# Query rotation from an SBUF copy, and the carried attention sums moved behind it, in a transformer layer of eight cores

## What is computed

```
xn = layernorm(x)
Q  = rope(xn @ W_q)            # 16 heads
K  = rope(xn @ W_k)            # 4 heads, each used by 4 query heads
V  = xn @ W_v
attn = softmax(Q K^T / sqrt(128)) V @ W_o
ffn  = (silu(xn @ w_gate * s_gate) * (xn @ w_up * s_up)) @ w_down * s_down   # int8 weights, inner width 8192
out  = x + attn + ffn
```

## Time and profile before

| | us |
|---|---|
| median of the two runs shown | 5281.77 |
| the two runs | 4993.61 and 5569.93 |
| the profiled execution | 4927.06 |
| span of its slowest core (core 7) | 4925.5 |
| spans of its eight cores | 4895.3 to 4925.5 |
| TensorE busy in that span | 4116.9 (84%) |
| VectorE busy | 1008.2 (20%) |
| ScalarE busy | 824.4 (17%) |

### The profile page before, as it was taken

How to read it: one execution, slowest core, us unless ns; L and a number is a source line. 1 busy time by engine, 2 the same in 40 slices (tenths; PEclk the granted TensorE clock), 3 DMA queues, 4 the chain that set the end, 5 groups by cost and what they waited for, 6 DMA issues and landing times.

```text
span 4925.5 us, 43667 instructions; the slowest of 8 cores (4895.3 to 4925.5 us)
## 1 busy us (share of the span) xinstructions
PE 4116.9 (84%) x18032; PEld 1774.3 (36%) x18032; DVE 1008.2 (20%) x1324; ACT 824.4 (17%) x659; POOL 224.7 (5%) x432
## 2 busy tenths in 40 slices
PE   0286666666666766799999999999999999999999
PEld 0032222222222222244444444444444444444444
DVE  2354333343233432111100111100111000111000
ACT  3203333333333333211100011000010000001000
POOL 0000000000000000000000000000000000000000
PEclk9998788887888878899999999999999999999999
DMA  9700000000000000443345633345633355533354
GB/s 144 181 1 12 10 9 11 10 12 11 9 10 11 10 9 5 165 175 152 150 151 180 222 154 154 154 154 185 222 150 150 131 184 192 188 154 154 116 187 149
DMA packets 139171, 545.03 MB, mean 111 GB/s; under 512 B 43824, under 2 KB 68416, under 8 KB 95584
## 3 DMA queue, kind: packets, MB, share of 16 engines
q0 software_dynamic: 60720, 465.67, 27.1%
q1 hardware_dynamic: 78256, 76.56, 6.0%
HBM read 345.06 MB, written 33.55 MB: 77 GB/s over the span
## 4 chain that ended last, share of the span: by engine, by line
PE 76%; ACT 12%; DVE 6%; DMA 3%; issue 2%; DVEq 0%; ACTq 0%; POOL 0%; SPq 0%; POOLq 0%
PE ps_sc L581 18%; PE ps_av L627 18%; PE ps_sc L598 18%; ACT expT L469 11%; PE ps_sc L459 5%; PE ps_sc L406 5%; PE ps_sm L637 4%; PE ps_sm L369 2%; PE ps_av L356 2%; DMA x_t<-x_nat 2%; PE ps_sc L454 2%; DVE rb_sb L380 1%; DMA wv_sb<-wv 1%; ACT sqt L276 1%; PE ps_av L326 1%
## 5 line engine op out<-in xcount | busy, mean ns | idle before, releaser
L581 PE MATMUL ps_sc<-xn_t,wg_sb 128*128 128x512 bf16 x4096 | 927.7, 380 | 25.3 <-DMA xn_t<-xn_scr 25.3
L598 PE MATMUL ps_sc<-xn_t,wu_sb 128*128 128x512 bf16 x4096 | 925.8, 379 | 0.0
L627 PE MATMUL ps_av<-fuse,wd_sb 128*128 128x512 bf16 x4096 | 894.5, 379 | 4.3 <-DVE fuse L607 4.3
L469 ACT ACTIVATE expT<-ps_sc,bias_h,isq_sb 128x2048 bf16<-128x2048 f32 x256 | 526.7, 2057 | 709.4 <-PE ps_sc L454 709.4
L581 PEld LDWEIGHTS ps_sc<-xn_t,wg_sb 128*128 128x128 bf16 x4096 | 401.2, 98 | 510.2 <-issue 28.2
L589 ACT ACTIVATE gate_sb<-ps_sc,sg_sb 128x512 bf16<-128x512 f32 x256 | 175.9, 687 | 2417.2 <-PE ps_sc L581 2417.2
L627 PEld LDWEIGHTS ps_av<-fuse,wd_sb 128*128 128x128 bf16 x4096 | 400.5, 98 | 488.5 <-issue 6.2
L598 PEld LDWEIGHTS ps_sc<-xn_t,wu_sb 128*128 128x128 bf16 x4096 | 400.8, 98 | 483.3
L607 DVE SCALAR_TENSOR_TENSOR fuse<-ps_sc,su_sb,gate_sb 128x512 bf16<-128x512 f32 x256 | 192.2, 751 | 1597.2 <-PE ps_sc L598 1597.2
L459 PE MATMUL ps_sc<-qr,kr 128*128 128x512 bf16 x768 | 269.8, 471 | 192.3 <-ACT expT L469 192.3
L380 DVE RECIPROCAL rb_sb<-ps_sm 128x512 f32<-128x512 f32 x64 | 214.9, 3358 | 877.4 <-PE ps_sm L365 875.8
(11 more groups left out here) (66 smaller groups left out, 1309.7 us busy)
## 6 DMA issues: line engine op xcount, KB each, us to landing
wg_sb<-wg POOLq DMA_DIRECT2D x128, 1024.0 KB, 4.6
wu_sb<-wu POOLq DMA_DIRECT2D x128, 1024.0 KB, 6.6
wd_sb<-wd POOLq DMA_DIRECT2D x64, 2048.0 KB, 7.4
wo_sb<-wo POOLq DMA_DIRECT2D x64, 512.0 KB, 6.7
x_t<-x_nat POOLq DMA_DIRECT2D x16, 1024.0 KB, 11.6
xT_sb<-xT SPq DMA_DIRECT2D x64, 256.0 KB, 6.0
outT<-out_sb SPq DMA_DIRECT2D x64, 256.0 KB, 5.9
wq_sb<-wq POOLq DMA_DIRECT2D x16, 512.0 KB, 5.1
```

What stands on the lines that cost most here:

```text
L469: exp_b[b] = es(lambda s, p=qp, b0=4 * b: s.activation(expT[p][:, b0:b0 + 4, :], ps_sc[:, :, :], AF.Exp, bias=bias_h[:], scale=isq_sb[:]), ...
L581: t_.matmul(PS(b), wg_sb[p][:, d, j:j + 128], xn_t[tp][:, d, :], start=(d == 0), stop=(d == DC - 1)))
L598: t_.matmul(PS(b), wu_sb[p][:, d, j:j + 128], xn_t[tp][:, d, :], start=(d == 0), stop=(d == DC - 1)))
L627: t_.matmul(PS(b), wd_sb[p][:, i, :], fuse[:, i, :], start=(i == 0), stop=(i == IC - 1)))
```

## The change

The query part rotates from a copy in SBUF. After the square, ScalarE copies the projected tile from its PSUM bank into a new bf16 buffer `qps`, and that copy is what frees the bank. VectorE waits for the copy and rotates with a new function `rope_sb`, which does the six operations of `rope` on `qps`. Since its inputs are both in SBUF, the odd half's tables are taken from partitions 64 to 127, so `cos_sb` and `sin_sb` grow to 128 partitions and are loaded twice each. K still uses `rope`.

In the same lines the block that put the carried sums and their epilogue into the query part is gone. `pend` stays set through it, and the score loop, which is not edited, finds it set at q = 0 also.

```diff
-            cos_sb = sba("cos_sb", [64, S], F32)
-            sin_sb = sba("sin_sb", [64, S], F32)
+            cos_sb = sba("cos_sb", [128, S], F32)
+            sin_sb = sba("sin_sb", [128, S], F32)
...
-            dma("y", "cs", lambda y: y.dma_start(cos_sb[:], cosd))
-            dma("y", "cs", lambda y: y.dma_start(sin_sb[:], sind))
+            dma("y", "cs", lambda y: y.dma_start(cos_sb[0:64, :], cosd))
+            dma("y", "cs", lambda y: y.dma_start(cos_sb[64:128, :], cosd))
+            dma("y", "cs", lambda y: y.dma_start(sin_sb[0:64, :], sind))
+            dma("y", "cs", lambda y: y.dma_start(sin_sb[64:128, :], sind))
...
+            qps = sba("qps", [128, 4, 512], BF16)
...
+            def rope_sb(src, dst_e, dst_o, t0):
+                ev(lambda v, p=src, a=t0: v.tensor_mul(
+                    tmp0[:], p[0:64, :], cos_sb[0:64, a:a + TS]))
+                ev(lambda v, p=src, a=t0: v.tensor_mul(
+                    tmp1[:], p[64:128, :], sin_sb[64:128, a:a + TS]))
+                ev(lambda v, d=dst_e: v.tensor_sub(d, tmp0[:], tmp1[:]))
+                ev(lambda v, p=src, a=t0: v.tensor_mul(
+                    tmp0[:], p[0:64, :], sin_sb[0:64, a:a + TS]))
+                ev(lambda v, p=src, a=t0: v.tensor_mul(
+                    tmp1[:], p[64:128, :], cos_sb[64:128, a:a + TS]))
                 return ev(lambda v, d=dst_o: v.tensor_add(d, tmp0[:], tmp1[:]))
...
-                    ew("v", st_, qp)
-                    ew("v", ss, sqd)
-                    qrope[t] = rope(ps_sc[:, t, :],
-                                    qr[0:64, t * TS:t * TS + TS],
-                                    qr[64:128, t * TS:t * TS + TS], t * TS)
-                    psum_free[t] = (sv, qrope[t])
-                    if pend is not None:
-                        emit_avsums_batch(pend, t)
-                        if t == NT - 1:
-                            emit_attn_epilogue(pend, pend_head[0],
-                                               pend_head[1])
-                            pend = None
+                    evv = es(lambda s, tt=t: s.copy(
+                        qps[:, tt, :], ps_sc[:, tt, :]), chain=False)
+                    psum_free[t] = (ss, evv)
+                    ew("v", ss, evv)
+                    qrope[t] = rope_sb(qps[:, t, :],
+                                       qr[0:64, t * TS:t * TS + TS],
+                                       qr[64:128, t * TS:t * TS + TS], t * TS)
```

More of the change, by code:

```diff
@@ L259, in rope @@
                 ev(lambda v, p=psum, a=t0: v.tensor_mul(
-                    tmp0[:], p[0:64, :], cos_sb[:, a:a + TS]))
+                    tmp0[:], p[0:64, :], cos_sb[0:64, a:a + TS]))
                 ev(lambda v, p=psum, a=t0: v.tensor_mul(
-                    tmp1[:], p[64:128, :], sin_sb[:, a:a + TS]))
+                    tmp1[:], p[64:128, :], sin_sb[0:64, a:a + TS]))
                 ev(lambda v, d=dst_e: v.tensor_sub(d, tmp0[:], tmp1[:]))
                 ev(lambda v, p=psum, a=t0: v.tensor_mul(
-                    tmp0[:], p[0:64, :], sin_sb[:, a:a + TS]))
+                    tmp0[:], p[0:64, :], sin_sb[0:64, a:a + TS]))
                 ev(lambda v, p=psum, a=t0: v.tensor_mul(
-                    tmp1[:], p[64:128, :], cos_sb[:, a:a + TS]))
+                    tmp1[:], p[64:128, :], cos_sb[0:64, a:a + TS]))
+                return ev(lambda v, d=dst_o: v.tensor_add(d, tmp0[:], tmp1[:]))
+            def rope_sb(src, dst_e, dst_o, t0):
+                ev(lambda v, p=src, a=t0: v.tensor_mul(
+                    tmp0[:], p[0:64, :], cos_sb[0:64, a:a + TS]))
+                ev(lambda v, p=src, a=t0: v.tensor_mul(
+                    tmp1[:], p[64:128, :], sin_sb[64:128, a:a + TS]))
+                ev(lambda v, d=dst_e: v.tensor_sub(d, tmp0[:], tmp1[:]))
+                ev(lambda v, p=src, a=t0: v.tensor_mul(
+                    tmp0[:], p[0:64, :], sin_sb[0:64, a:a + TS]))
+                ev(lambda v, p=src, a=t0: v.tensor_mul(
+                    tmp1[:], p[64:128, :], cos_sb[64:128, a:a + TS]))
                 return ev(lambda v, d=dst_o: v.tensor_add(d, tmp0[:], tmp1[:]))
```

## The result

The changed kernel's profiled execution took 4815.85 us against 4927.06, 111 us or 2.3% less. The changed kernel's executions lie close together (4815.85 to 4819.06 in the first set). Their ratio to those of the kernel before was 0.9738, with a 95% interval of 0.964 to 0.9836, wide because of one execution of the kernel before at 4993.61. That interval alone does not tell 2% from less. So the kernel is faster by 2.2%.

A forecast was written before the change was run, and what follows sets the result against it. VectorE's rotations were taken to bound the attention loop's query part. Per head -6.66 + 0.6 - 0.3 = -6.36 us, -95.4 over 15 heads; with 3 at the start, 4927 - 92 = 4835 us, range 4785 to 4935.

The forecast's parts named there:

- the copy and the rotation from it: In the query part: ScalarE's 64 copies hide in its idle time, and rotating from SBUF makes no difference.
- 4.26: Us of each head's path taken by the epilogue, reciprocal and product, standing ahead of the shift on VectorE.
- The query part: First projection to spreading matmul: 28.42 us as in the first head, in place of 35.08, 6.66 us less a head.
- a TensorE slower by up to a microsecond a tile would not show: Query part: VectorE is the bound at 5.78 us a tile, against TensorE's 4.77.
- q = 0: Stretch now holding the 32 carried matmuls: 0.3 to 1.05 us more than 17.17, taken as 0.6.
- the lower bound: For q = 0: 0.3 us more, with the clock rising as at the start of q = 1.
- The first batch's price at the front: Start of q = 0: the first batch of sums costs 2.5 us, given back by the raised clock.
- The start of q = 1: Entered at full clock, no longer at 1.2 GHz: 0 to 1.87 us less, taken as 0.3.
- The start of the kernel: Two more table loads of 512 KB: nothing to 13.3 us more, taken as 3.
- One bound: Rotation from the copy: at most 10 ns or so added, 1 us in all for 64 tiles.
- The rival of quicker rotations: Rotations run quicker on bf16: 4.1 us a head, 16 heads, 66 us, giving 4769 us; 5 in 100.
- the two rivals with a clock that stays down: q = 0 stays slow: about 4926 us, 5 in 100; query part slow too: 5083 us, 3 in 100.

## Why the mechanism was right, and the forecast gain too small

The forecast was 4835 us, 1.9% less, with 0.54 for a result within 2% and 0.42 for a faster one. It came out 2.2% faster, on the side with the smaller chance. The mechanism was right: the query part without sums takes what the first head's takes (28.38 us, or up to 0.35 more, in twelve of fifteen heads; forecast 28.42), the 32 matmuls are nearly free in q = 0, the clock rises there, the copy and the rotation from it cost nothing in the loop, and moving the epilogue alone gave 62 us in a run of its own, 4.1 us a head where 4.26 had been read.

The sum was too small: -92 us forecast, -111 measured on the two profiled executions. By its terms:

- The query part, "35.08 - 28.42 = 6.66 us less a head". This is the step that failed, and the reason is the head that I read: its clock was taken for that of all heads. Nine of the fifteen later heads of the kernel before have 36.76 us or more, since the first projection runs partly at 1.2 GHz (5.30 us and not 3.61); the mean of heads 2 to 15 is 36.08. In the changed kernel it is 28.79, with three such heads. The term is 7.29, not 6.66: 10 us in all. The prediction also held that a TensorE slower by up to a microsecond a tile would not show. At the first tile it shows in full, because VectorE has nothing to do until that projection is done: 30.06 - 28.38 = 1.68 us, where the projection takes 5.30 - 3.61 = 1.69 more. The prediction had looked at one query part, where the group of the lines would have told: 1024 projections of L406 had 397 ns on average, and 379 at full clock.
- q = 0, "I take 0.6". It measured 0.13, and the head shown above 0.26: the lower bound, taken from the start of q = 1, was the right row even though the idle time here is longer. 7 us in all. The first batch's price at the front was given as 2.5 us, which is what the distances give back; by the prediction's own rows it is 0.55 + 4.72 - 2.47 = 2.8.
- The start of q = 1, -0.3, measured -0.41. The starts of q = 2 and q = 3, which I had left alone, gave 0.23 back. Together 2 us the other way.
- The start of the kernel, +3. Between the two slowest cores of the profiled executions the first projection came 1.5 us earlier, not later; between averages over cores some 5 us later. 4.5 us, and not more than the scatter of cores. The experiments leave this term open.

10 + 7 - 2 + 4.5 is the missing 19 us. One bound was also short: 10 ns on each of the four products from the copied tile are 2.6 us in 64 tiles, not 1; nothing of it came true.

Why so many query parts of before had the low clock at their start, and few of the changed kernel, is not explained. In the kernel with only the epilogue moved, every later one has it. What the runs show is the price: a start at the low clock costs up to 1.7 us wherever it stands, 5.30 against 3.61 us at the projection and 16.71 against 15.02 at q = 2, where the first 4 us have a granted clock of about 0.6 in the long ones and 1.00 in the short ones. And the falls seem to trade between neighbours: with only the epilogue moved, q = 2 takes 15.02 in thirteen of fifteen heads while every later query part has the slow start. That one brings the other is not shown.

The rival of quicker rotations fell, at 684 and 687 ns. So did the two rivals with a clock that stays down: q = 0 has 0.87, and the query part 1.00 in the head shown, as far as TensorE works in it; in three heads only the start of the first projection ran at the low clock. The clock of q = 0 was 0.87 with the sums and 0.53 where they were taken out again. The Trainium skill, page "TensorE: Matmul & The Clock Gate", section "What's actually happening", says that activity releases the throttle, and these two numbers agree with it.

## What to carry to other kernels

Look at what stands ahead of the one operation that the next stage waits for, on its own engine's list: here a reciprocal and a product, 4.3 us together in each of 15 heads, were 1.2% of this kernel, and moving them cost nothing. Work moved to a stretch in which TensorE ran at the low clock and waited in short gaps was nearly free here, 32 matmuls for 0.13 us, because it raised the clock; but take the mean over all the repetitions before pricing such a move, since one repetition may be the lucky one. A copy that frees a buffer was worth nothing until the order made use of the freed buffer.

## What was not expected of the hardware

Adding 36 matmuls whose result nobody reads made the kernel faster, by 18 us on the cores' average: 2.1 us at the first exponential of most heads, 1.8 on average over q = 0, of which 0.8 was lost again at the query parts. And the same 32 matmuls, in TensorE's 9 us of idle time, were worth no more than in q = 0 itself, where they raise the clock from 0.53 to 0.87.
